# One TensorE-bound transformer block: fewer warming products, another order of VectorE and GpSimd in the opening, and a reordered last step

## What is computed

```
xn = layernorm(x)                              # [8, 256, 256]
q, k, v, g = xn@Wq.T, xn@Wk.T, xn@Wv.T, xn@Wg.T  # 16 heads of 128; rope on q and k
s  = clip(xn@Ws1.T@Ws2.T + bs2, -32, 32)       # 16 heads of 64 slots
z  = cumlogsumexp(s, over tokens); es = exp(s); enz = exp(-z)
A  = tril(q@k.T * scale)
qv = softmax(enz * (A@es))
o  = tril((qv*enz)@es.T) @ v
attn = (rms_norm(o) * g_norm * silu(g)) @ Wo.T
ffn  = (gelu(xn@Wgate.T) * (xn@Wup.T)) @ Wdown.T  # 4-bit weights, dequantised, 2048 wide
out  = x + attn + ffn
```

## Time and profile before

| | |
|---|---|
| median of three runs | 1087.41 us (1087.01 to 1087.88) |
| the profiled execution | 1087.74 us, of which the span is 1086.0 us |
| mean granted clock of TensorE | 0.998 |
| busy: PE, DVE, ACT, POOL | 1072.1, 920.1, 653.7, 420.3 us |

### The profile page before, as it was taken

One profiled execution on the slowest core, in us unless ns is written; L12 is line 12 of the kernel. 1 busy time (PEld: TensorE's weight loads), 2 busy tenths in 40 slices (PEclk: granted clock), 3 DMA queues, 4 the chain that ended last, 5 costly groups with the idle time before them and its releaser, 6 DMA issues.

```text
span 1086.0 us, 20566 instructions
## 1 busy us (share of the span) xinstructions
PE 1072.1 (99%) x7176; PEld 923.7 (85%) x7176; DVE 920.1 (85%) x1680; ACT 653.7 (60%) x2111; POOL 420.3 (39%) x308
## 2 busy tenths in 40 slices
PE   8899999999999999999999999999999999999998
PEld 7688888888888888888888888888888888888887
DVE  6898988888888888889888898889888889888886
ACT  4666565666655666565756556656565666656653
POOL 5353252433523355232642316343253432524331
PEclk9999999999999999999999999999999999999999
DMA  5020000200002000020000200002000010000001
GB/s 171 1 78 4 1 2 1 75 6 1 1 1 81 1 2 1 2 80 2 1 1 2 80 2 2 1 1 80 1 1 1 15 67 1 1 2 1 20 21 40
DMA packets 9542, 23.06 MB, mean 21 GB/s; under 512 B 864, under 2 KB 5856, under 8 KB 8544
## 3 DMA queue, kind: packets, MB, share of 16 engines
q1 hardware_dynamic: 9440, 21.76, 5.8%
HBM read 19.66 MB, written 2.10 MB: 20 GB/s over the span
## 4 chain that ended last, share of the span: by engine, by line
PE 92%; DVE 2%; issue 1%; ACT 0%; POOL 0%; POOLq 0%; DVEq 0%
PE bank L219 21%; PE bank L221 21%; PE bank L220 21%; PE bank L389 5%; PE bank L319 5%; PE bank L360 3%; PE bank L332 3%; PE bank L398 3%; PE bank L321 2%; PE bank L309 2%; PE bank L382 1%; PE bank L335 1%; PE bank L369 1%; PE bank L344 1%; PE bank L351 1%
## 5 line engine op out<-in xcount | busy, mean ns | idle before, releaser
L1437 POOL TENSOR_TENSOR inter_lo<-ffb,inter_hi 128x512 fp32r<-128x512 f32 x62 | 79.5, 1306 | 447.5 <-ACT inter_hi L791 447.5
L1428 POOL TENSOR_TENSOR qkT<-ra,xs 128x512 f32<-128x512 f32 x128 | 165.6, 1295 | 132.2 <-DVE xs L1101 108.8
L754 ACT ACTIVATE sm<-bank,mx 128x64 f32<-128x64 f32 x256 | 76.5, 326 | 144.9 <-DVE mx L1057 144.9
L1101 DVE TENSOR_TENSOR xs<-xs,rope 128x512 f32<-128x512 f32 x128 | 130.4, 1019 | 0.0
L735 ACT ACTIVATE xs<-bank 64x512 f32<-64x512 f32 x128 | 76.3, 596 | 75.4 <-PE bank L221 46.6
L1098 DVE TENSOR_TENSOR ra<-bank,rope 128x512 f32<-128x512 f32 x128 | 87.9, 687 | 36.4 <-ACT xs L736 34.6
L1046 DVE RECIPROCAL enzT<-enzT 128x256 f32<-128x256 f32 x64 | 111.6, 1744 | 0.0
L219 PE MATMUL bank<-xh,wgu_hi 128*128 128x512 f32 x256 | 105.4, 412 | 0.0
L219 PE MATMUL bank<-xh,wqk_hi 128*128 128x512 f32 x256 | 102.8, 402 | 1.1 <-DVE ffa L1082 1.1
L219 PE MATMUL bank<-wvg_hi,xh 128*128 128x512 f32 x256 | 101.0, 394 | 1.0 <-ACT xh L795 1.0
L221 PE MATMUL bank<-xh,wgu_lo 128*128 128x512 f32 x256 | 101.0, 395 | 0.0
(11 more groups left out here) (165 smaller groups left out, 3064.1 us busy)
## 6 DMA issues: line engine op xcount, KB each, us to landing
raw<-in_w_qkvg SPq DMA_DIRECT2D x7, 1024.0 KB, 7.4
scaled<-in_w_scaled SPq DMA_DIRECT2D x8, 640.0 KB, 8.5
packed<-in_w_packed SPq DMA_DIRECT2D x8, 384.0 KB, 3.1
acc<-in_x SPq DMA_DIRECT2D x4, 512.0 KB, 8.4
out<-acc SPq DMA_DIRECT2D x3, 512.0 KB, 3.0
raw<-in_w_qkvg SPq DMA_DIRECT2D x2, 512.0 KB, 6.7
ws_raw<-in_w_slot SPq DMA_DIRECT2D x8, 48.0 KB, 2.9
rope<-in_rope_tab SPq DMA_DIRECT2D x1, 256.0 KB, 8.0
```

What stands on the lines that cost most here:

```text
L754: ins = act.activation(sm[:, c], src[:, c], ACT.Exp, bias=mx[:, g:g + 1], accum_out=ssum[:, g:g + 1])
L1101: dve.tensor_tensor(two(xs[i % 2][:, :]), two(xs[i % 2][:, :]), sin, ALU.mult).then_inc(sin_done, 1)
L1428: pool.tensor_tensor(qkT[:, i, :], ra[i % 2][:, :], xs[i % 2][:, :], ALU.add).then_inc(roped, 1)
L1437: pool.tensor_tensor(dst[1][e], ffb[e][:, :], dst[0][e].bitcast(F32), ALU.subtract).then_inc(inter_lo, 1)
```

## The change

The number of warming products goes from 24 to 15. The first token load is issued as two DMAs of two tiles each, and the statistics of tiles 2 and 3 wait for the second. In the opening the lists of four engines get another order: the second decoding pass goes ahead of the scaling of the second tokens, the third and fourth behind their low parts; GpSimd starts the low part of the query and key weights only when the second tokens are scaled, does its four rotations before it dequantises the MLP weights, and dequantises only after the first sum over slots; its two mask selections stand later; some steps of VectorE and ScalarE trade places. In step 1 TensorE does the output products of the second sequence before it waits for the transposes of pair 3, and its neighbours follow. In the last step both norms stand ahead of the first gating; the last share of step 30's tokens is copied out of PSUM by ScalarE and added by GpSimd; and `last_outputs` is divided into products that need the high parts and products that need the low parts.

```diff
 SLOT_K = 3 * GROUP
-WARM = 24
+WARM = 15
 W_VG, W_QK, W_GU, W_OD = range(4)
...
 first = w_qkvg[0].rearrange("p (k n) -> p k n", k=KT)
-load_x(0)
+sp.dma_start(acc[:, 0:2, :], x_rows[:, 0:2, :]).then_inc(x_in[0], 16)
+sp.dma_start(acc[:, 2:NT, :], x_rows[:, 2:NT, :]).then_inc(x0_rest_in, 16)
 sp.dma_start(raw_k[:, :, 512:1024], first[:, :, 512:1024]).then_inc(raw0_in, 16)
...
 for bp in range(BP - 1):
-    sp.wait_ge(acc_done, 2 * ((HP - 1) * BP + bp + 1))
+    if bp < BP - 2:
+        sp.wait_ge(acc_done, 2 * ((HP - 1) * BP + bp + 1))
+    else:
+        sp.wait_ge(acc_done, 2 * LAST - 1)
+        sp.wait_ge(share_added, 1)
     sp.dma_start(out_rows[:, bp * NT:(bp + 1) * NT, :],
...
 rows = slice(LAST_BP * NT + i, LAST_BP * NT + i + n)
-sp.wait_ge(acc_done, 2 * LAST + k + 1)
+sp.wait_ge(acc_done, 2 * LAST + k)
 sp.dma_start(out_rows[:, rows, :], acc[:, rows, :]).then_inc(out_sent, 16)
...
-def last_outputs(i, stop):
+def last_outputs_hi(i):
...
     for s in (0, 1):
-        mm = three(pe, last_out(i), [ogT[u][s][:, cols] for u in range(2)],
-                   [w[:, s, :] for w in wod], False, stop and s == 1)
-    if stop:
-        mm.then_inc(out_full, 1)
+        for w in wod:
+            pe.matmul(last_out(i), ogT[0][s][:, cols], w[:, s, :], start=False, stop=False)
+def last_outputs_lo(i):
+    cols = slice(i * P, (i + 1) * P)
+    for s in (0, 1):
+        mm = pe.matmul(last_out(i), ogT[1][s][:, cols], wod[0][:, s, :], start=False,
+                       stop=i > 0 and s == 1)
+    return mm
...
 mlp_up(0, 0, 0, 2)
-slot_softmax(0, rg[1])
 pe.wait_ge(G_ready, 8)
 mlp_up(0, 0, 0, 3)
+slot_softmax(0, rg[1])
 pe.wait_ge(ff_gelu, 1)
...
 slot_rows(st)
+outputs(st, 1, php, st + 1)
 if prep:
...
     transpose_x(prep, 1, sc[0])
-outputs(st, 1, php, st + 1)
 project_vg(st + 1, nbp, nhp, 3, True)
...
 last_transpose(1)
-for i in range(NT):
-    pe.wait_ge(last_hi, i // 2 + 1)
-    pe.wait_ge(last_lo, i // 2 + 1)
-    last_outputs(i, i > 0)
+pe.wait_ge(last_hi, 1)
+last_outputs_hi(0)
+last_outputs_hi(1)
+pe.wait_ge(last_lo, 1)
+last_outputs_lo(0)
+last_outputs_lo(1).then_inc(out_full, 1)
+for i in (2, 3):
+    pe.wait_ge(last_hi, 2)
+    last_outputs_hi(i)
+    pe.wait_ge(last_lo, 2)
+    last_outputs_lo(i).then_inc(out_full, 1)
...
 swap_halves(0, 1)
-slot_exp(0, 0)
 swap_halves(0, 2)
-split_hi(0, W_GU)
+slot_exp(0, 0)
 swap_halves(0, 3)
-inner_copy(1, rg[1])
 off_diagonal(0, 0)
 off_diagonal(0, 1)
+inner_copy(1, rg[1])
 copy_v(1, 1, 0)
...
 copy_v(1, 1, 2)
+split_hi(0, W_GU)
 copy_state(0)
...
 act.wait_ge(gn_half, 1)
-softmax_exp(0)
 gate_square(0, 0)
+softmax_exp(0)
 gate_tanh(0, 0)
...
     x_hi(prep, 0, sc[0])
-    x_hi(prep, 1, sc[0])
 softmax_exp(st)
+if prep:
+    x_hi(prep, 1, sc[0])
 copy_v(st + 1, npar, 2)
...
     ins.then_inc(ms_done, 1)
+act.wait_ge(out_full, 2 * st)
+act.activation(ffa[0][:, :], pj[3][:, :], ACT.Copy).then_inc(share_off, 1)
 for b in range(2):
     act.wait_ge(ogT_full, 2 * st + b + 1)
-    if b == 0:
-        act.wait_ge(out_full, 2 * st)
     for h in range(2):
...
 for i in range(NT):
+    if bp == 0 and i == 2:
+        dve.wait_ge(x0_rest_in, 16)
     dve.bn_stats(bns[:, i, :], acc[:, bp * NT + i, :]).then_inc(bn_done, 1)
...
 decode(0, 0)
+decode(0, 1)
 gate_g(0, 0, 0)
...
 gate_g(0, 0, 1)
-decode(0, 1)
 gate_g(0, 0, 2)
-decode(0, 2)
 gate_g(0, 0, 3)
...
 x_lo(1, 1, sc[0])
-decode(0, 3)
+decode(0, 2)
 slot_lo(0)
-dve.wait_ge(const_in, 32)
-dve.wait_ge(consts, 1)
+decode(0, 3)
 inner_lo(0, rg[0])
 decode(0, 4)
+dve.wait_ge(const_in, 32)
+dve.wait_ge(consts, 1)
 rope_cos(0, 0)
...
 rope_sin(0, 2)
-cumulate(0, 0)
+score_diagonal(0, 0)
+score_diagonal(0, 1)
 rope_cos(0, 3)
 rope_sin(0, 3)
 inner_lo(1, rg[1])
-score_diagonal(0, 0)
-score_diagonal(0, 1)
-invert(0, 0, 0)
 gate_g(1, 1, 0)
+cumulate(0, 0)
 score_diagonal(0, 2)
 score_diagonal(0, 3)
-invert(0, 0, 1)
+invert(0, 0, 0)
 gate_g(1, 1, 1)
+gate_g(1, 1, 2)
+invert(0, 0, 1)
 softmax_in(0, 0, rg[0])
 clip(1, 1, sc[0][:, :])
-gate_g(1, 1, 2)
 gate_g(1, 1, 3)
 softmax_max(0)
+gate_arg(0, 0)
 x_stats(2)
 cumulate(1, 1)
+gate_gelu(0, 0)
+hidden(0, 0)
 x_bias(2)
 softmax_inverse(0)
-gate_arg(0, 0)
 slot_query(0, 0, rg[1])
-gate_gelu(0, 0)
-hidden(0, 0)
 gate_arg(0, 1)
...
 if prep:
-    x_lo(prep, 1, sc[0])
     invert(st + 1, npar, 0)
 add_share(st, pbp, 0, rg[1])
+if prep:
+    x_lo(prep, 1, sc[0])
 if bp == 1 and more:
...
 slot_query(st, par, rg[1])
-rope_cos(st + 1, 0)
-rope_sin(st + 1, 0)
 if prep:
     inner_lo(prep, sc[0])
+rope_cos(st + 1, 0)
+rope_sin(st + 1, 0)
 rope_cos(st + 1, 1)
...
 last_norm(0)
-last_gate(0)
 last_norm(1)
-add_share(st, LAST_BP - 1, 1, pj[3])
+last_gate(0)
 last_gate(1)
...
 pool.wait_ge(const_set, 4)
-for m in (mask_a, mask_w):
-    ins = pool.affine_select(out=m[:, :, :], in_=m[:, :, :], compare_op=ALU.is_ge, fill=0.0, base=0,
-                             pattern=[[0, 2], [1, P]], channel_multiplier=-1)
-ins.then_inc(consts, 1)
...
                        ALU.subtract).then_inc(w_lo if k else vg0_lo, 1)
+for m in (mask_a, mask_w):
+    ins = pool.affine_select(out=m[:, :, :], in_=m[:, :, :], compare_op=ALU.is_ge, fill=0.0, base=0,
+                             pattern=[[0, 2], [1, P]], channel_multiplier=-1)
+ins.then_inc(consts, 1)
 pool.wait_ge(ws1_hi, 1)
...
 x_pow(1)
+pool.wait_ge(xn_done, 2)
 split_lo(0, W_QK)
+rotate(0, 0)
+rotate(0, 1)
+rotate(0, 2)
+rotate(0, 3)
+pool.wait_ge(scan_done, 2)
 dequantise(0, W_GU)
-for i in range(4):
-    rotate(0, i)
 split_lo(0, W_GU)
...
     pool.tensor_tensor(rstd[:, c], mse[:, c], mhalf[:, c], ALU.pow).then_inc(pow_done, 1)
+pool.wait_ge(share_off, 1)
+pool.wait_ge(scal_done, STEPS + 1)
+a = acc[:, (LAST_BP - 1) * NT + 2:LAST_BP * NT, :].rearrange("p n c -> p (n c)")
+pool.tensor_tensor(a, a, ffa[0][:, :], ALU.add).then_inc(share_added, 1)
```

More of the change, by code:

```diff
@@ L136, in build @@
         x_in = [sem(f"x_in{i}") for i in range(BP)]
+        x0_rest_in = sem("x0_rest_in")
         raw_in, packed_in, scaled_in, ws2_in = sem("raw_in"), sem("packed_in"), sem("scaled_in"), sem("ws2_in")
@@ L177, in build @@
         last_hi, last_lo = sem("last_hi"), sem("last_lo")
+        share_off, share_added = sem("share_off"), sem("share_added")
         out_rows = out.rearrange("b (n p) d -> p (b n) d", p=P)
@@ L834, in _ @@
             swap_halves(0, 1)
+            swap_halves(0, 2)
             slot_exp(0, 0)
-            swap_halves(0, 2)
-            split_hi(0, W_GU)
             swap_halves(0, 3)
-            inner_copy(1, rg[1])
             off_diagonal(0, 0)
             off_diagonal(0, 1)
+            inner_copy(1, rg[1])
             copy_v(1, 1, 0)
@@ L854, in _ @@
             act.wait_ge(gn_half, 1)
+            gate_square(0, 0)
             softmax_exp(0)
-            gate_square(0, 0)
             gate_tanh(0, 0)
@@ L910, in stage @@
                     x_hi(prep, 0, sc[0])
+                softmax_exp(st)
+                if prep:
                     x_hi(prep, 1, sc[0])
-                softmax_exp(st)
                 copy_v(st + 1, npar, 2)
@@ L1184, in _ @@
             x_lo(1, 1, sc[0])
+            decode(0, 2)
+            slot_lo(0)
             decode(0, 3)
-            slot_lo(0)
+            inner_lo(0, rg[0])
+            decode(0, 4)
             dve.wait_ge(const_in, 32)
             dve.wait_ge(consts, 1)
-            inner_lo(0, rg[0])
-            decode(0, 4)
             rope_cos(0, 0)
@@ L1202, in _ @@
             inner_lo(1, rg[1])
-            score_diagonal(0, 0)
-            score_diagonal(0, 1)
-            invert(0, 0, 0)
             gate_g(1, 1, 0)
+            cumulate(0, 0)
             score_diagonal(0, 2)
             score_diagonal(0, 3)
+            invert(0, 0, 0)
+            gate_g(1, 1, 1)
+            gate_g(1, 1, 2)
             invert(0, 0, 1)
-            gate_g(1, 1, 1)
             softmax_in(0, 0, rg[0])
             clip(1, 1, sc[0][:, :])
-            gate_g(1, 1, 2)
             gate_g(1, 1, 3)
             softmax_max(0)
+            gate_arg(0, 0)
             x_stats(2)
             cumulate(1, 1)
+            gate_gelu(0, 0)
+            hidden(0, 0)
             x_bias(2)
             softmax_inverse(0)
-            gate_arg(0, 0)
             slot_query(0, 0, rg[1])
-            gate_gelu(0, 0)
-            hidden(0, 0)
             gate_arg(0, 1)
@@ L1298, in stage @@
                 slot_query(st, par, rg[1])
+                if prep:
+                    inner_lo(prep, sc[0])
                 rope_cos(st + 1, 0)
                 rope_sin(st + 1, 0)
-                if prep:
-                    inner_lo(prep, sc[0])
                 rope_cos(st + 1, 1)
@@ L1381, in _ @@
             last_norm(0)
+            last_norm(1)
             last_gate(0)
-            last_norm(1)
-            add_share(st, LAST_BP - 1, 1, pj[3])
             last_gate(1)
@@ L1407, in split_lo, with dequantise @@
                 pool.tensor_tensor(dst, src, hi.bitcast(F32), ALU.subtract).then_inc(w_lo, 1)
```

(4 more changed lines are left out.)

## The result

| | before | after |
|---|---|---|
| time, median (range), us | 1087.46 (1087.01 to 1087.88) | 1080.89 (1080.65 to 1081.48) |
| ratio, 95% interval | | 0.9941 (0.9929 to 0.9953) |
| profiled execution: time, span, mean clock | 1087.74, 1086.0, 0.998 | 1081.48, 1079.7, 1.000 |
| TensorE busy | 1072.1 | 1067.8 |

What follows compares the result with a forecast made beforehand. TensorE, busy 1072.1 of 1086.0 us, was taken as the bound. Opening 5.0, step 1 1.1 and end 1.7 sum to 7.8 off 1087.74; with the median 0.33 lower, 1079.6 us, range 1077.6 to 1082.6.

Steps and rivals of the forecast that it cites:

- The first projection: Opening: shorter warming and the split first load bring the first `wvg` product from 12.26 to 10.8, 1.5 us earlier.
- The second tokens: Opening: holding back GpSimd's low part shortens VectorE's scalings from 3.44 to 1.38 us and removes TensorE's wait, 1.5 us.
- The rotations: Opening: rotations ahead of dequantising cut the scores' wait of 2.3 to 0.5 to 0.6, 1.7 us gained.
- The clock: Opening: without the long wait before the scores, the clock's fall to 0.50 has no cause, 1.7 us gained.
- Given back: Opening: new waits cost 0.4 us before the first `mlp_up` and 1.0 us at GELUs and third tokens' low part.
- Step 1: Step 1: output products ahead of the second transposes remove a wait of 1.0 and a small one, 1.1 us.
- The end: Last step: earlier second gating, no wait for the last gating, last product and share 1.7 us earlier.
- 1 (VectorE's list): VectorE's list bounds the opening, each `rope_sin` pays 1.3, GELU waits grow by 1: gain 5.5, 1081.9 us; chance 0.17.
- 2 (a second fall): The clock falls again somewhere, or rises later because warming is short: 1081.3 us; chance 0.10.
- 3: Estimated waits given back are absent and small gaps behind waits close: gain 9.8, 1077.6 us; chance 0.13.
- 4: Slower: dequantised weights hang on late sums and delay `mlp_up`; 1090.4 us if sums end at 45; chance 0.03.
- 5: VectorE and GpSimd still collide elsewhere; only warming, step 1 and the last step give: 1083.7 us; chance 0.05.

Runs made afterwards that it cites:

- one load: Changed kernel with the first tokens loaded in one DMA again, without the wait for the rest; 15 warming products kept: 1083.33 us.
- step 1 put back: Changed kernel with the whole of step 1 in its old order, opening and end still changed: 1080.47 us.
- second tokens' load first: Changed kernel with the second tokens' load issued ahead of the query and key weights', and scales prepared after those tokens' high parts: 1080.92 us.
- end alone: Kernel before with only the last step's changes (norm order, share through ScalarE and GpSimd, divided last outputs): 1085.78 us.
- dequantising first: Changed kernel with GpSimd dequantising ahead of the four rotations again, without waiting for the sums: 1083.20 us.

## Why the prediction came out as it did

- **The first projection (1.5)**: right, 1.50 and 1.76 in the two profiles. Single parts taken back cost 0.5 (warming, by the gains) and 0.5 (load, in the two executions at a clock of 1.000); in sum less than the term, since the other stays. That nothing is lost by the shorter warming is borne out in the changed kernel alone: with one load, three of five executions lost about 2 more.
- **The second tokens (1.5)**: right, 3.03 - 1.50 = 1.53. The scalings took 1.38 as worked out, and undoing the wait alone costs 1.3. "No slack" was right too, but the place that I took for safe was not: the second tokens' load lands at 12.1 in some executions, where a wait of 0.96 comes back, and the scores start 0.76 later.
- **The rotations (1.7)**: 1.53 (4.56 - 3.03), waiting left 0.66, and one of the four `rope_sin` of step 0 pays 0.8, all as forecast. The Trainium skill's rule ("SBUF — State Buffer", "SBUF: two separate sides") says that every one that starts under a rotation pays. All rows here agree with that, and of the three others none started under one, or only at its very end.
- **The clock (1.7)**: right for the profiled execution, wrong for the median. Between the two profiles the fall's absence gives 6.20 - 4.56 = 1.64. But half of the executions before have no fall, and the others are only 0.56 slower. The step that fails is "here I count it whole": I had taken the range of three times (0.87 us) for proof that all had the fall, where it could as well mean that the fall costs less than that. Why 1.64 in the rows is 0.56 in the time is argued, not shown: the wait of 1.1 for a GELU that followed it would be longer without the fall, since VectorE and ScalarE, whose pace does not hang on that clock (`rope_sin` takes 0.68 at 32.13, in the slow stretch, as elsewhere), set its end. No execution before at a clock of 1.000 was profiled.
- **Given back (0.4 and 1.0)**: the 0.4 is right, 6.14 - 5.73 = 0.41, at `okz`; for `wgu_lo` there is no wait. The 1.0 is the term that was too large: 5.73 - 5.22 = 0.51. The GELU waits are 0.5 and 0.3, not 0.7 and 1.1, and the third tokens' low part 0.7, not 0.3. So the opening gave 5.2 between the two profiles with 5.0 forecast: this half less given back stands against 0.17 less at the rotations and some 0.1 in the rest.
- **Step 1 (1.1)**: the step that failed most. The waits of 1.0 and 0.2 went as said, and 1.2 for `Wt` came; the part is worth 0.0 in the traces, and taking it back costs nothing. I had priced the products that move and not the one line that moves on VectorE: `inner_lo` ahead of the first `rope_cos` puts the second `rope_sin` under GpSimd's rotation. I had applied the rule of held-up instructions to the opening alone. With that line back, the rest of the part is worth 0.7 (0.68 in the trace and 0.75 in the medians, against "step 1 put back"), so even then the 1.1 was too large: the wait for the slots' low part, 0.2 before, is 0.7 there.
- **The end (1.7)**: right: 1.8 in the trace, 1.79 as an experiment of its own.
- The rivals: 1 (VectorE's list) fits the end of step 0 and step 1, not the opening's first terms. 2 (a second fall) is seen in none of the nine executions of the changed kernel, but a mean clock below 1.000 is there in three of five with one load and in one with the second tokens' load first, each some 2 to 3 us slower. 3 had half of what is given back right, but not its gain of 9.8. 4 and 5 are out: `mlp_up` starts at 38.9 to 39.7, and the scalings are 1.38.

The forecast was 1079.6, the median is 1080.89: 1.3 us apart. Between the two profiles, 1087.74 and 1080.73, the gain is 7.0 where 7.8 were forecast; step 1 lacks 1.06 of it, and the opening (0.2) and the end (0.1) gave more than forecast. The other part is the clock: the profiled execution before had the fall and stands 0.3 to 0.4 above its median, and I took the whole 7.8, clock included, from the median. The count fits: 1087.72 - 1080.70 = 7.02 against the executions with the fall, 1087.16 - 1080.70 = 6.46 against those without. The parts taken back one by one cost 0.5, 0.5, 1.3, 2.5 and 1.8. That this makes 6.6, the whole gain, means little: the second 0.5 leaves out the three slower executions with one load, with which it is 2.3, and parts that share a wait need not add up.

## What to carry to other kernels

Where an instruction of one engine is held up beside another engine's work, as `rope_sin` is here, price every move on either against every instruction that it newly overlaps, the small ones too. Here it paid to put an instruction that reads PSUM under GpSimd's rotation and the two-input SBUF one behind it; moving the `rope_sin` alone let its successor pay. Before a stretch at a lower clock is counted as lost time, split the executions by their mean clock and compare the medians: a wait behind the stretch can hide part of its loss, and the rows of one profile do not show how much. And once waits are small, look at how long the late engine has worked without a gap: three of the four orders tried here behind the opening only moved the wait.

## What the runs showed of the hardware

- A `rope_sin` (two SBUF operands of 128x512) that starts during one GpSimd operation of 1.27 to 1.29 with 0.23 to 0.92 of it left took 0.78 to 1.47, the more the more was left; under two such operations in a row (2.96 together) it took up to 1.50; with 0.13 or less left, or alone, 0.68. `rope_cos` and the slots' low part, which read a PSUM bank, keep 0.68 beside one. A reciprocal of 128x256 took 1.74 to 1.75 with and without GpSimd.
- The second tokens' load, issued at 3.1, was there at 12.1 in one execution of the changed kernel and by 11.4 in another; in a kernel with the same loads it was there by 10.9.
- In the programs with 15 warming products, their 30 records took between 4.96 and 6.00 in different executions; with the two rates of the earlier trace rows, the clock's first rise comes at different times too, though the column shows 1.00 throughout.
- Of the four programs whose profile has a standstill of 2.0 to 2.3 (the kernel before, "end alone", "dequantising first", "one load"), some executions show a mean clock below 1.000 and some do not. In "second tokens' load first", with none above 1.35 behind the warming, one of four does.
- The executions below 1.000 are slower by 0.56 (before) and 0.64 ("end alone") in the median, by 0.9 with dequantising first, and by some 2 or more with one load (1083.3 to 1084.2 against 1081.4 and 1081.5) and with the second tokens' load first (1082.9 against 1080.8): a fall has no one price.
